# Moving two steps' shared-expert work out of the feed phase of a two-layer decoder kernel

## The chip, the cores and the metric

The kernel runs on one core of a Trainium2 chip. A core has five engines that run their own instruction streams and wait for each other on semaphores: TensorE (PE) multiplies matrices, VectorE (DVE) and ScalarE (ACT) work on tiles, GpSimd (POOL) issues indirect DMAs and does small elementwise work, and SyncE (SP) issues most of the other DMAs. PE's clock has two levels, 1.2 and 2.4 GHz; the profile shows the granted one as a share of 2.4 GHz. The metric is the device time of one launch in microseconds (us), lower is better.

## The reference, cut to what matters

The input is 4 batches of 1024 tokens with 256 features, all in fp32. Two layers run one after the other, each with a first attention, a cross attention over 77 context rows, and a mixture of experts; a layer norm follows each of the three. Only the mixture of the first layer matters here:

```
probs = softmax(x @ router_w + router_b);  tw, ti = top_k(probs, 8)      # of 64 experts
routed = sum over experts e of  cw[:, e] * (silu(x @ w1[e] + b1[e]) @ w2[e] + b2[e])
shared = sum over 2 shared experts of  silu(x @ sw1 + sb1) @ sw2 + sb2   # 256 -> 512 -> 256
x = layernorm(x + routed + shared)
```

## The kernel before, in words

The 1024 positions are cut into 8 steps of 128 positions, and a step holds those positions of all 4 batches: 512 tokens. Four phases follow each other in one instruction stream per engine.

The **first attention** (`attention_phase`, layer 0) is a software pipeline. `SEQUENCE0` lists the jobs of a round with how many rounds a step lies behind; `steady` rolls it out, so that round n works on step n for the front of the chain and on step n - 3 for its end. Rounds 8 to 10 only drain. A job has a PE part that fills a PSUM bank and an ACT or DVE part that empties it: `v`, `qk`, `kt`, `ret`, `mix`, `up` are the first attention, `wo` its output, `x1t`, `mx`, `mt`, `sc`, `pv`, `wout` the cross attention, `x2t`, `rt`, `rank` the routing, `cwt` and `b2` the experts' bias; `put` is 32 indirect DMAs on POOL that scatter a step's rows into lists by expert (L597). SP writes zeros into the lists ahead of them (L486), loads inputs, and stores each step's rows (`x2s`, L493).

The **shared experts** are cut into units. A unit is one block of 128 of the 1024 hidden features for one step: `inward` (L110, 2 matmuls of 512 columns, 4 records in the trace), a Silu on ACT (L118) and `outward` (L127, 4 matmuls of 256 columns, 8 records), which adds into PSUM over the 8 units of a step. There are 8 units in a step and 64 in all. `with_units` puts the first step's 8 units into rounds 9 and 10.

The **feed** (`feed_phase`) does the routed experts: 80 quads of 4 pages of 128 rows. A quad is a 512 KB load from the lists (L1504), 8 transposes (L1716), 16 first matmuls (L1728), 8 second matmuls (L1739), weights copied by DVE (L1633, L1638), and a 512 KB store (L1508). `feed_order` writes the order of all engines: 20 units ahead of the first quad (`FIRST_UNITS`), then one unit behind four of five quads from quad 24 on until unit 64; behind 6 of 7 quads from quad 26 on one of the 64 "sums", which add one eighth of a step's gathered results (POOL gathers L1441, DVE adds L1456). When a step's 8 units are done, DVE adds them to the step's rows (`base`, L1697), SP stores those (`send_base`, L1517) and loads the next (L1513). The first `send` also issues the load of `w2` (L1520, twice 4 MB). All of this stands in SP's order ahead of the loads of the first quad. The other weights `w1` (4 MB, L2133) are loaded at the start of the kernel.

The **second attention** (layer 1) begins when the last quad's results are stored. Its DVE and POOL streams first do 3 of the 18 sums left by the feed (`LATE`), the other 15 and the last norm are put by `with_late` behind jobs of rounds 0 to 5. The last phase, layer 1's mixture, is not touched.

Of the kernel before, what the change touches and what calls it, by code (L numbers as in the profile page):

```python
# [26 lines left out]
K0 = 8  # L27
# [5 lines left out]
TOTAL = STEPS * UNITS  # L33
# [44 lines left out]
class SharedExperts:  # L78
# [16 lines left out]
    def load_rows(self, sp, src_t, s):  # L95
        for b in range(NB):
            at = b * SEQ + s * P
            sp.dma_start(self.sx[:, s % 2, :, b * P:(b + 1) * P],
                         src_t[:, at:at + P].rearrange("(c p) n -> p c n", p=P)).then_inc(self.sx_in[s % 2], 16)

    def inward(self, nc, pe, n, sp_h):
        s, u = n // UNITS, n % UNITS
        if n == 0:
            pe.wait_ge(self.sw1_in, 16 * ES)
# [16 lines left out]
    def outward(self, nc, pe, n, sp_y):  # L121
        u = n % UNITS
        if n == 0:
            pe.wait_ge(self.sw2_in, 16)
# [40 lines left out]
def steady(sequence):  # L165

    order = []
    for n in range(STEPS + max(ahead for _, ahead, _ in sequence)):
        for stage, ahead, part in sequence:
            if 0 <= n - ahead < STEPS:  # L170
# [33 lines left out]
def bank_jobs(order):  # L204
# [5 lines left out]
    ("wout", 2, 0), ("wout", 2, 1), ("cwt", 3, 0), ("put", 3, 1), ("qk", 0, 0), ("x1t", 1, 0), ("x1t", 1, 1),  # L210
# [17 lines left out]
def attention_phase(nc, sems, shared, layer, d, src, src_t, dst, dst_t, experts, prefetch, lists, slots, weights, page_ends,  # L228
                    spare=None, route=None, block=None,
                    over=(), kept=(), late_on_pool=None, late_on_vector=None, units=None):  # L230
# [17 lines left out]
    with ExitStack() as ctx:  # L248
# [61 lines left out]
        if first:  # L310
# [25 lines left out]
            qt = x1t  # L336
        else:
            xt, qt = (units.sw2[:].rearrange("p (k c n) m -> p k c (n m)", k=2, c=KC)[:, k] for k in range(2))
# [26 lines left out]
            placed = sb("placed", [P, NB, K1, E])  # L365

# [20 lines left out]
        if first:  # L387
# [3 lines left out]
            blank = [sem(f"blank{i}") for i in range(STEPS)]  # L391
        else:
# [63 lines left out]
        def _(sp):  # L456
# [23 lines left out]
            prefetch(sp, 0)  # L480
            if first:
                sp.wait_ge(pool_ready, 3)
            out_rows = dst.rearrange("(b s) n -> s b n", b=NB)
            for n in range(STEPS + 3 if first else 0):
# [3 lines left out]
                if n == 1:  # L488
                    sp.dma_start(units.sb1[:], d["sb1"]).then_inc(units.sb1_in, 16)
                if 0 <= n - 3 < STEPS:  # L490
# [15 lines left out]
                if n + 2 < STEPS:  # L506
                    filled(sp, ("v", n, 1))
                    filled(sp, ("qk", n, 3))
                    load_t(n + 2)
                if n == STEPS - 1:  # L510
# [7 lines left out]
                    sp.wait_ge(sent_cols, 64 * 2)  # L518
                    for k in range(2):
                        units.load_rows(sp, dst_t, k)  # L520
                if 0 <= n - 2 < STEPS:
# [3 lines left out]
                    sp.dma_start(route[n - 2, 0], place[:].rearrange("p b e -> p (b e)")).then_inc(sent_place, 16)  # L525
            for n in range(0 if first else STEPS + 3):
# [88 lines left out]
        def _(act):  # L615
            def move(out, in_, job):
                empties(nc.scalar.activation(out, in_, ACT.Copy), job)

            begin_here(act)
            for dst_ap, src_ap in others:  # L620
                act.dma_start(dst_ap, src_ap).then_inc(consts, 16)
            if not first:
                act.wait_ge(consts, CONSTS)
                nc.scalar.activation(small[:, 0:1], gate[:], ACT.Exp, scale=-1.0).then_inc(gate_exp, 1)
            for job in order:
                stage, i, p = job
                pair = slice(2 * p, 2 * p + 2)
                if stage == "unit":
                    units.activate(nc, act, i, wide[:, 0])
                if stage in ("v", "kt"):  # L630
# [56 lines left out]
        def _(dve):  # L687
# [81 lines left out]
            if not first:  # L769
                lay_out()  # L770
            for job in order:
# [151 lines left out]
                if stage == "rank":  # L923
# [38 lines left out]
                    if i + 1 < STEPS:  # L962
                        dve.wait_ge(mask_done, i + 1)
                        step(nc.vector.tensor_copy(counts[:, 0], counts[:, NB]))
                if stage == "b2":
# [8 lines left out]
        def _(pe):  # L974
# [16 lines left out]

            begin_here(pe)
# [17 lines left out]
            for job in order:  # L1010
# [3 lines left out]
                if first and job == ("mx", 0, 0):  # L1014
                    pe.wait_ge(ready, READY)
                if stage == "unit":
# [213 lines left out]
                if stage == "rank":  # L1230
# [6 lines left out]
                    fills(ins, job)  # L1237
                if stage == "cwt":
# [986 lines left out]
```

## Time and profile before

| | us |
|---|---|
| timed runs | 1865.97, 1873.0, 1875.45; median 1873.0 |
| profiled execution, first to last instruction | 1981.9 |
| profiled execution's own time beside its span | the page gives none |
| PE / DVE / ACT / POOL busy in it | 1687.5 / 1165.2 / 623.2 / 892.7 |
| mean granted clock of PE | 0.922 |
| DMA traffic | 322.61 MB, mean 163 GB/s |

The page cuts the span into 40 slices of 49.5 us. The first attention takes slices 1 to 12, the feed ends near 1105 us, the second attention near 1560 us, and the last phase takes the rest. In the feed's slices PE is busy 8 to 9 tenths and the DMA engines 8 to 9 tenths as well. The chain of work that ended last is 68% PE, 10% DVE, 6% DMA and 6% issue.

### The profile page before, as it was taken

Reading aid. Unit: us, or ns where it says so; the run is one execution under the profiler, and the core shown is the slowest. Engines: PE = TensorE matmul, PEld = TensorE weight load, DVE = VectorE, ACT = ScalarE, POOL = GpSimd, SP = SyncE. Lnnn points to the kernel's source line nnn. Section 1 sums busy time; section 2 is a strip of 40 time slices with the busy share of each in tenths; the row PEclk is TensorE's granted clock in tenths of the full one; section 3 lists DMA queues with packets and bytes.
Section 4 is the critical chain, followed back from the end, with each engine's and each line's share of the span. In section 5 each row is a group of like instructions: output and inputs, shape, how many; then the busy total and the mean of one; then the engine's idle time right before and its main releaser. Section 6 shows DMA issues by size and latency. Waiting matters only on the chain.

```text
span 1981.9 us, 45543 instructions
## 1 busy us (share of the span) xinstructions
PE 1687.5 (85%) x17739; PEld 1329.8 (67%) x17739; DVE 1165.2 (59%) x3228; ACT 623.2 (31%) x957; POOL 892.7 (45%) x1000
## 2 busy tenths in 40 slices
PE   6788888887689889998998478889977599999994
PEld 4566665666566567666676355667666499999994
DVE  4576655665432177776656456788765245655564
ACT  1232322222231277454555223445432111111110
POOL 0017556655758102888888856333323102222223
PEclk9999989998689999999998779999987699999997
DMA  9416543555448899888998922113111512333332
GB/s 325 150 46 199 184 150 116 190 169 191 146 147 237 219 304 295 285 278 273 297 294 290 317 78 82 57 65 121 69 39 65 164 49 76 91 94 98 98 94 69
DMA packets 269634, 322.61 MB, mean 163 GB/s; under 512 B 25083, under 2 KB 245487, under 8 KB 268655
## 3 DMA queue, kind: packets, MB, share of 16 engines
q1 hardware_dynamic: 234559, 226.38, 36.1%
q0 software_dynamic: 33024, 92.32, 14.4%
q8 instruction: 144, 2.36, 0.5%
q10 hardware_dynamic: 1840, 1.00, 0.2%
q14 instruction: 67, 0.55, 0.1%
HBM read 157.22 MB, written 162.40 MB: 161 GB/s over the span
## 4 chain that ended last, share of the span: by engine, by line
PE 68%; DVE 10%; issue 6%; DMA 6%; ACT 4%; POOL 3%; another core or an unknown queue 2%; SPq 1%; DVEq 1%; POOLq 0%; ACTq 0%
PE wide L2067 13%; PE d_yp L2079 6%; PE wide L110 4%; PE wide L127 4%; PE wide L1199 4%; PE wide L1202 3%; PE wide L1728 3%; PE e_yp L1739 3%; PE wide L1186 3%; PE bank L1033 3%; PE bank L1212 3%; PE bank L1219 2%; PE e_xp L1716 2%; PE bank L1105 2%
## 5 line engine op out<-in xcount | busy, mean ns | idle before, releaser
L1441 POOL DMA_INDIRECT big<-results,slots x256 | 263.4, 1029 | 202.1 <-DMA results<-e_y 125.5
L2067 PE MATMUL wide<-d_xt,d_ws 128*128 128x128 f32 x2272 | 279.0, 277 | 0.6 <-issue 0.6
L2067 PEld LDWEIGHTS wide<-d_xt,d_ws 128*128 128x128 f32 x2272 | 272.7, 193 | 4.5 <-issue 1.0
L597 POOL DMA_INDIRECT lists<-big,slots x160 | 159.6, 997 | 116.7 <-DVE slots L961 70.3
L663 ACT ACTIVATE pt<-wide 77x2048 f32<-77x2048 f32 x64 | 119.8, 1871 | 196.5 <-PE wide L1202 118.7
L1936 POOL DMA_INDIRECT d_picked<-results,slots x64 | 64.0, 1001 | 182.0 <-DMA results<-d_y 168.7
L1967 ACT ACTIVATE d_gate<-wide 128x512 f32<-128x512 f32 x71 | 42.4, 597 | 323.9 <-PE wide L2067 323.9
L2079 PE MATMUL d_yp<-d_wd,d_h 128*128 x568 | 134.2, 379 | 0.0
L1456 DVE SCALAR_TENSOR_TENSOR big<-big,weights 128x256 f32<-128x256 f32 x256 | 108.9, 487 | 41.6 <-DMA big<-results,slots 28.2
L110 PE MATMUL wide<-shared_sx,shared_sw 128*128 128x512 f32 x256 | 126.3, 616 | 7.7 <-DMA shared_sx<-res_t 5.2
L127 PEld LDWEIGHTS wide<-shared_sw,shared_sh 128*128 128x128 f32 x512 | 97.3, 191 | 45.1 <-issue 29.6
L127 PE MATMUL wide<-shared_sw,shared_sh 128*128 128x256 f32 x512 | 121.4, 380 | 3.6 <-DVE big L1697 3.6
L158 POOL TENSOR_TENSOR rest_ones<-rest_ones 128x4 f32<-128x4 f32 x108 | 121.0, 1120 | 2.0
L554 POOL TENSOR_TENSOR rs<-mv,eps 128x4 f32<-128x4 f32 x32 | 6.4, 199 | 234.9 <-DVE mv L712 234.1
L1212 PE MATMUL bank<-pt,vals 77*32 77x128 f32 x2048 | 89.6, 293 | 25.3 <-issue 15.4
L2079 PEld LDWEIGHTS d_yp<-d_wd,d_h 128*128 128x128 f32 x568 | 102.6, 190 | 11.0
L1998 DVE COPY d_ws<-big 128x1024 f32 x142 | 92.3, 693 | 27.5 <-issue 26.4
L2016 DVE TENSOR_TENSOR d_h<-d_gate,wide 128x512 f32<-128x512 f32 x71 | 48.7, 686 | 97.7 <-PE wide L2067 97.7
L1587 ACT ACTIVATE e_xt<-e_xp 128x1024 f32<-128x1024 f32 x80 | 81.9, 1024 | 76.5 <-PE e_xp L1716 48.7
L1716 PE MATMUL e_xp<-e_ident,e_x 128*128 128x128 f32 x640 | 86.9, 280 | 15.8 <-DMA e_x<-lists 12.2
L1199 PE MATMUL wide<-x1t,keys 32*77 32x128 f32 x1024 | 69.7, 315 | 35.8 <-issue 13.6
L1728 PE MATMUL wide<-e_xt,e_w1s 128*64 128x128 f32 x1280 | 89.4, 283 | 12.5 <-DVE e_w1s L1633 11.0
(280 smaller groups left out, 3488.8 us busy)
## 6 DMA issues: line engine op xcount, KB each, us to landing
lists<-zero SPq DMA_DIRECT2D x20, 2048.0 KB, 14.6
e_x<-lists SPq DMA_DIRECT2D x80, 512.0 KB
results<-e_y SPq DMA_DIRECT2D x80, 512.0 KB
d_x<-lists SPq DMA_DIRECT2D x71, 128.0 KB
results<-d_y SPq DMA_DIRECT2D x71, 128.0 KB
e_w<-in_L_w SPq DMA_DIRECT2D x2, 4096.0 KB
shared_sw<-in_x_t SPq DMA_DIRECT2D x32, 128.0 KB
x<-in_x SPq DMA_DIRECT2D x8, 512.0 KB
```

Source lines behind the costliest of these rows:

```text
L110: ins = nc.tensor.matmul(sp_h, self.sw1[:, c, u * P:(u + 1) * P], self.sx[:, s % 2, c], start=c == 0, stop=c == KC - 1)
L127: ins = nc.tensor.matmul(sp_y[b // 2][:, b % 2 * DM:(b % 2 + 1) * DM], self.sh[:, n % 2, b * P:(b + 1) * P], self.sw2[:, u], start=u == 0 ...
L158: step(self.nc.gpsimd.tensor_tensor(self.ones[:, 1], self.ones[:, 0], self.ones[:, 0], ALU.pow))
L597: pool.indirect_dma_start(out=lists, out_offset=bass.IndirectOffsetOnAxis(ap=slots[:, b, i, k:k + 1], axis=0), in_=z2[i % 3][:, b, :], in_ ...
L663: empties(nc.scalar.activation(pt[0:CTX, p % 2].rearrange("k (j n) -> k j n", j=4), ps[0:CTX], ACT.Exp, scale=score_scale), job)
L1199: mm(out[0:CTX, r, n * P:(n + 1) * P], keys[quarter(r), p, c, h * CTX:(h + 1) * CTX], qt[quarter(r), c, toks(p)], start=True, stop=False, ...
L1212: ins = mm(out[quarter(r), at:at + P], vals[:, p, c * 8 + 2 * r + h], pt[0:CTX, p % 2, of:of + P], start=True, stop=True)
L1441: pool.indirect_dma_start(out=picked[:, c % NG, b, :], out_offset=None, in_=results[0:-(-PAGES_OF_STEP[s] // 4) * 4 * R0, :], in_offset=ba ...
L1716: ins = tr(xp[:, h, (a * KC + c) * P:(a * KC + c + 1) * P], x[:, j % NX, h, a, c * P:(c + 1) * P], ident[:])
L1728: ins = mm(hp[h * H0:(h + 1) * H0, a * R0:(a + 1) * R0], w1s[:, j % NW1, h, a, c], xt[:, j % 2, h, a, c], start=c == 0, stop=c == KC - 1)
L2067: ins = mm(out[T % 2][:, a * P:(a + 1) * P], ws[:, T % NW, n, c, a * P:(a + 1) * P], xt[:, T % 2, c], start=c == 0, stop=c == KC - 1)
L2079: ins = mm(yp[T % 2][:, 0:DM], h[:, T % 2, c * P:(c + 1) * P], wd_flat[:, bass.ds(e * (HC * DM) + c * DM, DM)], start=c == 0, stop=c == HC ...
```

## The change: what it does

The first step leaves the units: its 8 units become 8 jobs `win` (inward and Silu) and 4 jobs `wtwo` (outward for two batches and four units each) of the first attention, all in round 8 except two `wtwo` in round 9. They use the four narrow PSUM banks, and DVE adds their result to a copy of the step's rows (`gbase`), which SP stores. Their weights are loaded in round 1 into the memory that `w1` had; so the load of `w1` moves from the start to the end of SP's round 9, behind the last `wtwo`.

The other seven steps have 56 units. The first 8 stay in rounds 9 and 10, 13 (was 20) come ahead of the first quad, and the feed goes on to unit 48; units 49 to 55 and the last outward run on PE behind the last quad, ahead of the second attention, where DVE then adds them and SP stores them. So quads 59 to 79 have no unit, where 70 to 79 had none. The sums come behind 7 of 9 quads instead of 6 of 7, and 22 (was 18) are left to the second attention, whose `xt` and `qt` get memory of their own.

```diff
+SOON = 1
+FOUR = UNITS // 2
+GROUPS = SOON * UNITS // FOUR
+TOTAL = (STEPS - SOON) * UNITS
+IN_FEED = TOTAL - UNITS
...
-    behind = [("x0t", 0, 1), ("sig", 0, 0)]
+    behind = [("x0t", 0, 1), ("sig", 0, 0), ("num", 0, 1), ("x0t", 1, 1), ("sig", 1, 0)]
     for i in range(4):
-        behind += [("x1t", i, 1), ("q", i, 1), ("mx", i, 1), ("mx", i, 3)]
+        behind += [("num", i + 1, 1), ("x1t", i, 1), ("q", i, 1), ("mx", i, 1), ("mx", i, 3)]
...
+    ("wout", 2, 0), ("wout", 2, 1), ("wtwo", 9, 10), ("wtwo", 9, 11), ("win", 8, 0), ("cwt", 3, 0), ("put", 3, 1),
+    ("win", 8, 1), ("qk", 0, 0), ("x1t", 1, 0), ("x1t", 1, 1), ("win", 8, 2),
+    ("mx", 1, 0), ("ln2", 2, 0), ("qk", 0, 1), ("b2", 3, 0), ("b2", 3, 1), ("mx", 1, 1), ("win", 8, 3), ("res", 1, 0), ("put", 3, 2),
+    ("qk", 0, 2), ("x2t", 2, 0), ("x2t", 2, 1), ("mx", 1, 2), ("win", 8, 10), ("put", 3, 3), ("qk", 0, 3), ("mx", 1, 3),
+    ("win", 8, 11), ("put", 3, 4), ...
+    ("sc", 1, 0), ("wtwo", 8, 0), ("mix", 0, 0), ("top", 2, 0), ("ret", 0, 1), ("pv", 1, 0), ("sc", 1, 1), ("wtwo", 8, 1),
+    ("mix", 0, 1), ("up", 0, 0), ("rank", 2, 0), ("sc", 1, 2), ("pv", 1, 1), ("sc", 1, 3), ("win", 8, 12), ("pv", 1, 2),
+    ("win", 8, 13), ("pv", 1, 3),
...
-            prefetch(sp, 0)
             if first:
                 sp.wait_ge(pool_ready, 3)
+            else:
+                prefetch(sp, 0)
+                last_units.send(sp)
...
+                    sp.dma_start(gw2, d["sw2"].rearrange("e (c p) n -> p (e c) n", p=P)).then_inc(units.sw2_in, 16)
...
+                if n == 4:
+                    sp.wait_ge(sent_cols, 64)
+                    load_group(0)
+                    load_gbase(0)
...
+                if n == STEPS + 1:
+                    filled(sp, ("wtwo", GROUPS - 1, 1))
+                    prefetch(sp, 0)
+                    send_gbase(0)
...
+            if not first:
+                for n in range(IN_FEED + 1, IN_FEED + 3):
+                    units.activate(nc, act, n, wide[:, 0])
             begin_here(act)
             for dst_ap, src_ap in others:
                 act.dma_start(dst_ap, src_ap).then_inc(consts, 16)
             if not first:
+                for n in range(IN_FEED + 3, TOTAL):
+                    units.activate(nc, act, n, wide[:, 0])
...
             if not first:
+                last_units.add_base(dve)
                 lay_out()
...
+            if not first:
+                for n in range(IN_FEED + 1, TOTAL + 1):
+                    if n < TOTAL:
+                        units.inward(nc, pe, n, wide[:, 0])
+                    if n == IN_FEED + 1:
+                        last_units.begin(pe)
+                    units.outward(nc, pe, n - 1, [wide[:, 1], wide[:, 2]])
             begin_here(pe)
...
+                if stage == "win":
...
+                    for c in range(KC):
+                        ins = mm(out[:], gw1[:, c, u * P:(u + 1) * P], gx[:, c], start=c == 0, stop=c == KC - 1)
+                    fills(ins, job)
+                if stage == "wtwo":
+                    for n in range(FOUR):
+                        emptied(pe, ("win", i, n))
+                    for bb in range(2):
+                        for n in range(FOUR):
+                            u = i % 2 * FOUR + n
+                            ins = mm(out[:, bb * DM:(bb + 1) * DM], gh[:, u, toks(2 * p + bb)], gw2[:, u],
+                                     start=n == 0, stop=n == FOUR - 1)
+                    fills(ins, job)
...
-LATE = STEPS * K0 - 18
+LATE = STEPS * K0 - 22
 AHEAD = 3
-FIRST_UNITS = 20
+FIRST_UNITS = 13
...
-            if unit[0] <= TOTAL:
+            if unit[0] <= IN_FEED:
...
-        if j >= begun + 2 and (j - begun) % 7:
+        if j >= begun + 2 and (j - begun) % 9 < 7:
             sums(1)
```

## Rows read from the trace of the kernel before

**Rows 1.** Windows: length, busy PE, PEld, DVE, ACT, POOL; PE clock, DMA share, GB/s

```profile
417.80:485.00 67.20, 56.41 (x834) 42.46 (x831) 41.34 (x104) 18.66 (x25) 40.34 (x45) 0.92 0.60 192
485.00:558.40 73.40, 53.10 (x537) 39.78 (x534) 34.24 (x98) 15.40 (x19) 47.10 (x52) 0.68 0.61 202
...
685.00:767.00 82.00, 72.19 (x734) 55.27 (x736) 57.02 (x189) 59.72 (x91) 0.00 (x0) 1.00 0.91 294
...
986.00:1105.00 119.00, 106.69 (x821) 77.86 (x818) 71.62 (x262) 61.98 (x96) 98.06 (x95) 0.96 0.90 287
1105.00:1129.00 24.00, 0.03 (x1) 0.06 (x1) 7.58 (x23) 2.51 (x3) 19.43 (x21) 0.52 1.00 305
```

**Rows 2.** Groups by line of PE in round 7, 417.8 to 485

```profile
L1033 PE MATMUL bank<-shared_sw,wqk 128*128 128x512 f32 x16 | 7.8, 612 | 0.0
...
L1069 PE MATMUL bank<-shared_sw,state 128*32 128x128 f32 x64 | 5.3, 294 | 1.4 <-issue 1.3
L1074 PE MATMUL bank<-big,shared_sx 128*32 128x128 f32 x64 | 5.0, 281 | 0.7 <-issue 0.6
...
L1039 PE MATMUL bank<-wv,shared_sw 128*128 128x256 f32 x16 | 3.6, 379 | 0.0
```

**Rows 3.** Timeline of PE: last wout of the first attention, and two units ahead of quads

```profile
558.41 5.99 PE L1219 MATMUL bank<-wout,att_t 128*128 128x256 f32 x16
...
614.25 1.88 PE L110 MATMUL wide<-shared_sx,shared_sw 128*128 128x512 f32 x4
...
617.69 1.88 PE L110 MATMUL wide<-shared_sx,shared_sw 128*128 128x512 f32 x4
```

**Rows 4.** Chain of waits between the first attention and the first quad

```profile
597.41 2.95 DMA res<-x2s
...
611.07 1.30 DVE big L1697 x2
...
680.16 4.89 DMA e_x<-lists
```

**Rows 5.** Timeline of SP in the same stretch: start, time of issue

```profile
615.74 15.92 SPq L1520 DMA_DIRECT2D e_w<-in_L_w  x2
633.81 26.10 SPq L98 DMA_DIRECT2D shared_sx<-res_t  x4
659.96 2.23 SPq L1517 DMA_DIRECT2D mid<-big  x1
669.50 0.36 SPq L1513 DMA_DIRECT2D big<-res  x1
```

**Rows 6.** Timeline of POOL: the last scatter of the last step

```profile
654.00 0.96 POOL L1572 DMA_INDIRECT lists<-big,slots  x1 [0.30 <-issue]
```

**Rows 7.** Chain of waits in the feed's last third

```profile
1046.53 0.87 PE e_xp L1716 x8
1047.41 1.02 PE wide L1728 x16
...
1053.14 0.87 PE e_xp L1716 x8
...
1072.48 1.98 PE wide L1728 x16
```

**Rows 8.** Timeline of ACT, DVE and PE between the feed and the second attention

```profile
1117.58 1.28 ACT L624 ACT_TABLE_LOAD   x1 [11.52 <-issue]
...
1125.96 1.67 DVE L1456 SCALAR_TENSOR_TENSOR big<-big,weights 128x256 f32<-128x256 f32 x4 [5.36 <-DMA big<-mid]
...
1128.97 1.96 PE L1001 MATMUL bank<-pt,wk 128*128 128x77 f32 x8 [24.04 <-DMA memory<-in_L_norm]
```

**Rows 9.** Chain of waits in the second attention: its wout jobs

```profile
1279.13 1.92 PE bank L1219 x8
...
1324.72 1.92 PE bank L1219 x8
...
1365.46 1.92 PE bank L1219 x8
```

More of the change, by code:

```diff
@@ L169, in steady @@
         for stage, ahead, part in sequence:
-            if 0 <= n - ahead < STEPS:
+            if stage in ("win", "wtwo"):
+                if n == ahead:
+                    order.append((stage, part // 10, part % 10))
+            elif 0 <= n - ahead < STEPS:
                 order.append((stage, n - ahead, part))
@@ L489, in _ @@
                     sp.dma_start(units.sb1[:], d["sb1"]).then_inc(units.sb1_in, 16)
+                    sp.dma_start(gw2, d["sw2"].rearrange("e (c p) n -> p (e c) n", p=P)).then_inc(units.sw2_in, 16)
+                    for e in range(ES):
+                        sp.dma_start(gw1[:, :, e * HS:(e + 1) * HS], d["sw1"][e].rearrange("(c p) n -> p c n", p=P))\
+                            .then_inc(units.sw1_in, 16)
                 if 0 <= n - 3 < STEPS:
@@ L629, in _ @@
                     units.activate(nc, act, i, wide[:, 0])
+                if stage == "win":
+                    u, at = i % 2 * FOUR + p, i % 2 * FOUR + p
+                    if i == 0 and p == 0:
+                        act.wait_ge(units.sb1_in, 16)
+                    if i >= 2 and p == 0:
+                        filled(act, ("wtwo", i - 2, 1))
+                    ps = filled(act, job)
+                    empties(nc.scalar.activation(gh[:, at], ps[:], ACT.Silu, bias=units.sb1[:, u:u + 1]), job)
                 if stage in ("v", "kt"):
@@ L1015, in _ @@
                     pe.wait_ge(ready, READY)
+                if not first and job == ("mx", 0, 0):
+                    last_units.end(pe)
                 if stage == "unit":
@@ L1237, in _ @@
                     fills(ins, job)
+                if stage == "win":
+                    u = i % 2 * FOUR + p
+                    if i == 0 and p == 0:
+                        pe.wait_ge(units.sw1_in, 16 * ES)
+                        pe.wait_ge(units.sw2_in, 16)
+                    if i % 2 == 0 and p == 0:
+                        pe.wait_ge(gx_in, 64 * (i // 2 + 1))
+                    for c in range(KC):
+                        ins = mm(out[:], gw1[:, c, u * P:(u + 1) * P], gx[:, c], start=c == 0, stop=c == KC - 1)
+                    fills(ins, job)
+                if stage == "wtwo":
+                    for n in range(FOUR):
[6 more added lines that the diff above has]
+                    fills(ins, job)
                 if stage == "cwt":
@@ L1479, in norm, with begin, end, add_base @@
             ins.then_inc(out_done, 1)
+        class LastUnits:
+            def begin(self, pe):
+                pe.wait_ge(sy_used, STEPS - SOON - 1)
+            def end(self, pe):
+                pe.wait_ge(sy_used, STEPS - SOON)
+            def add_base(self, dve):
+                base_on_vector(dve, STEPS - SOON - 1)
+            def send(self, sp):
+                base_on_sync(sp, STEPS - SOON - 1)
+        def base_on_vector(dve, n):
+            dve.wait_ge(base_in, 16 * (n + 1))
+            dve.wait_ge(experts.out_full, n + 1)
+            for k in range(2):
+                pair = slice(2 * k, 2 * k + 2)
+                ins = nc.vector.tensor_tensor(base[:, pair], sp_y[k][:].rearrange("p (b n) -> p b n", b=2),
+                                              base[:, pair], ALU.add)
+            ins.then_inc(sy_used, 1)
+        def base_on_sync(sp, s):
+            sp.wait_ge(sy_used, s + 1)
+            sp.dma_start(out_by_step[(SOON + s) * P:(SOON + s + 1) * P], base).then_inc(base_sent, 16)
         def late_on_pool(pool, n):
```

84 lines of the change are left out of this document (54 added, 30 removed), and 5 rows, old and new, of the table SEQUENCE0.

## The prediction, written before the changed kernel ran

> **What bounds the kernel now.** I read the windows first, cut at the phases' ends, then PE's groups and timelines inside a phase, then the chain of waits and SP's timeline where PE stands still. Four stretches matter.
>
> Round 8 of the first attention is a drain: it lasts 73.4 us although PE has less to do than in round 7, which takes 67.2. PE is busy for 53.1 us of it, but at a granted clock of 0.68, against 56.4 us at 0.92 in round 7 [rows 1]. So this round is short of work, and its work runs slowly: what ends waits there is a chain through PE, ACT and DVE.
>
> Between the first attention and the first quad (the head, 596 to 685), PE does 20 units at 3.44 us each (617.69 - 614.25) [rows 3], but the first quad is not held by PE alone. SP stands in `w2`: issued at 615.74, it leaves no room in SP's queue for the next small load, whose issue takes 26.1 us, to 659.9. Only then come the store of a step's rows and its landing, at 669.5 [rows 5], another step's rows that wait for unit 24, and at 680.16 the first quad's load, 4.9 us [rows 4]. The scatters on POOL end at 655.0 [rows 6], so they are not what ends last.
>
> In the feed a quad with a unit takes 6.61 us (1053.14 - 1046.53) at the full clock [rows 7], and this is PE's own time. Quads without a unit are carried by the DMAs: the first 24 take 82.0 us at 294 GB/s and a DMA share of 0.91, with PE at 72.2 busy. The last third, 986 to 1105, moves 287 GB/s at 0.90 with PE busy for 106.7 of 119 us [rows 1]. So two limits lie close together there.
>
> From 1105 to 1129 PE does nothing [rows 1]; it waits 24.04 us for the second attention's constants [rows 8].
>
> **The change part by part.** The sum is against the profiled execution's span, 1981.9 us. The page gives no time around it, and the timed median is 1873.0, 5.5% below. Which stages the profiling stretches no view shows; I carry the difference over in microseconds.
>
> *Rounds 8 and 9.* Round 8 gets eight `win`, each the first half of a unit, 1.72 us, and two `wtwo` of 3.44: 13.8 + 6.9 = 20.7 us of PE. Round 7 has the jobs of round 8 and in their place `qk`, `v` and `mix`, which alone are 7.8 + 3.6 + 5.3 + 5.0 = 21.7 us [rows 2]. So round 8 becomes a round like 7, which is the nearest row: 67.2 + 1 for Silu's tables, about 5 us less than now. The `wout` behind it is at the low clock now, 5.99 us for 16 [rows 3], where 8 take 1.92 at the full one [rows 9]: 2 us more. Together -7. Ends: all 20.7 us on top and the clock as it is, +21; or 53.1 x 0.68 + 20.7 = 57 us and no idle, -16. Two more `wtwo` in round 9 put 6.9 us ahead of `rank`, of which I let 3 fall into waits: +4 for SP, nothing for POOL, whose scatters follow `wout`.
>
> *The early loads.* `w1` leaves the start, two smaller weights and a step's columns come. PE's work there never waits for them in the chain; I cost it at nothing, with 3 us either way if the saturated first stretch matters.
>
> *The head.* SP's `x2s` store is issued at 597.41 and lands in 2.95 [rows 4]; with -7 and +4 it is issued at 594.4. But now 4.19 MB of `w1` stand just ahead of it in SP's queue. At the 305 GB/s of a window with DMA share 1.00 [rows 1] that is 13.7 us; at the pace of `w2`, which takes 44.2 us (659.96 - 615.74) for twice as much beside the scatters [rows 5], 22. It is contiguous, so I take 14: it lands at 611.4. DVE's plan and the first base follow that store, now 12.0 us behind it (to 612.37) [rows 4], so 623.4, and `w2` 3.4 us later, 626.8. The scatters end at 648. Up to there `w2` moves 8.39 / 44.2 = 0.19 MB per us, 4.0 MB; the other 4.4 MB at 0.294 [rows 1] take 15: 663. The store of the second step's rows and its landing take 9.5 as now (669.50 - 659.96) [rows 5]: 672.5. With 13 units the third step's send is no longer ahead of the quads, so their load follows at 673 and lands at 678, against 685.05: -7 for the whole stretch up to the first quad. PE waits for the first base, then does 12 units, 41.3 us, until 665; it does not hold the quad. The seven units taken from here are 24 us of PE, but only the send counts. Ends: -18 with round 8 at its best, +14 with none of it hidden and `w1` at 22.
>
> *The feed's quads.* Quads 24 to 58 keep their pattern of units. Then 8.5 units leave the quads from 59 on: 29.2 us of PE. What is late next is the DMAs. That stretch moves 119 x 0.287 = 34.2 MB; two gathers and a step's rows in and out fewer, 2.6 MB, leave 31.6 MB, at the 294 GB/s of the unitless quads 107.5 us: -11.5. POOL, 98.1 us busy for the 18 sums there [rows 1], has 16, about 87, and is not the limit. Ends: -29 when the DMAs give way, and +13 when the clock falls (below).
>
> At this place the Trainium skill says otherwise: in DMA: Bandwidth & Descriptors, section Where 436 GB/s comes from, transfers between HBM and SBUF are held by the memory side at about 358 GB/s per core. By it the 31.6 MB would take 88 us (an estimate from that page) and the whole 29 us of PE would come out; the trace shows 294 at a share of 0.91, so I stay with that.
>
> *The change-over.* Seven inwards and eight outwards, 7.5 units or 25.8 us, go into PE's 24 us of waiting. They begin when PE ends, at 1104.9. The first three run; unit 52 needs the Silu of 51, which on ACT stands behind the wait for the last store and the issue of the constants, to 1117.6 [rows 8], so PE waits some 3 us: 1104.9 + 25.8 + 3 = 1134. The keys start there instead of 1128.97: +5. DVE's sums, up to 1127.6 [rows 8], are over by then; the last base is added at 1135, and the layout goes along with the keys. On SP the send of the last rows stands behind loads that are issued anyway. Ends: 0, if the warm clock gives the keys back, and +26, if none is hidden.
>
> *The late sums.* Two successive rounds of the second attention take 45.6 (1324.72 - 1279.13) and 40.7 us (1365.46 - 1324.72) [rows 9], the first with four more sums: 1.2 us each, so +4 for four. Each also puts a gather on POOL, but spread over five rounds. Ends +1 and +8.
>
> Sum: -7 - 11.5 + 5 + 4 = -9.5, so 1972.4 for the profiled span and **1863.5** for the median.
>
> **The rivals.**
>
> *The DMAs give way.* Without units the quads follow PE, and the feed loses all 29.2 us. For it: the last third is already at a share of 0.90 with PE nearly full, so the share is no proof of a limit. Against: the first 24 quads have no units and no gathers, and are at 294 GB/s. -7 - 29.2 + 5 + 4 = -27: 1846. The figure of the Trainium skill above would end there.
>
> *SP's queue eats the head.* `w1` moves at the pace of `w2`, 8 us more, and round 8 gains nothing, since its waits are of ACT's and DVE's making: the first quad comes 4 us later than now instead of 7 earlier. For it: 26.1 us of a small load's issue behind `w2` [rows 5]. Against: `w1` has long contiguous rows. +4 - 11.5 + 5 + 4 = +1.5: 1874.5.
>
> *The clock falls in the quads without units: slower.* PE has 3.2 us of work per quad (6.61 - 3.44) against 5.1 of the DMAs (107.5 / 21), and at 1072 to 1074 the trace has a stretch where the 16 first matmuls take 1.98 us instead of 1.02 [rows 7]. At the low clock a quad is 6.3 us of PE: 21 of them 132 us, not 107.5, and the units behind the last quad take twice 25.8. That is +50 for all of it. It decides from the point where the low level holds for a quarter of the stretch; at half, +25, the sum is +15.5: 1888.5. Against: in the first 24 quads PE is 88% busy and the clock stays at 1.00 [rows 1], so the fall feeds on waits longer than those.
>
> **How the numbers follow.** About 0.5%, 9.4 us, is what a measurement of this kernel can tell from no change. The forecast has 0.45, with an own range of 1853 to 1872 and somewhat more than half of it below 1863.6; the DMAs giving way 0.20, SP's queue 0.20, the clock 0.15. Faster by over 0.5%: 0.25 + 0.20 + 0.02 = 0.47. Within: 0.18 + 0.15 + 0.03 = 0.36. Slower: 0.02 + 0.03 + 0.12 = 0.17. The range takes in the first rival's 1846 and most of the third's way to 1888: 1845 to 1882.
>
> **What would show it.** Round 8 of the changed kernel at about 68 us with a granted clock near 0.9; `w1` issued just ahead of `x2s`, and that store landing some 14 us later behind it; the load of the first quad close behind the second base's store, some 10 us after the end of `w2` instead of 20; quads 59 to 79 at 5.1 us each with the DMA share at 0.9 or above; the keys some 29 us behind the last quad; rounds 2 to 4 of the second attention a little longer. The forecast is wrong if round 8 grows, if the quads from 59 on are below 4.5 or above 5.7 us, or if the units behind the last quad run at the low clock.

## The result, and the profile after

The changed kernel takes 1900.55 us (median of 4 runs, 1894.29 to 1903.04) against 1874.22 for the kernel before on the same chip: a ratio of 1.0149, 95% interval 1.0115 to 1.0183. It is slower by 1.5%, where 1863.5 was forecast, and outside the range that ended at 1882.

Its profiled execution has a span of 1900.4 us at 1902.2 us of device time, so 1.8 us lie around the span. That shows what was wrong with the profile of before: its span of 1981.9 lies 109 us above the timed median, because that execution was held up, by what no view shows. A second profile of the kernel before has a span of 1869.9, and it is the one to compare with. Of the 112 us between the two, 58 lie ahead of round 8 of the first attention, 24 between there and the last `x2s` store's issue, and 33 in the second attention, which the prediction read too [rows 9]. From the keys to the last phase, first in the profile that the prediction used, then in the second one (columns as in [rows 1]):

```profile
1128.97:1560.80 431.83, 344.59 (x4787) 256.20 (x4788) 295.88 (x955) 150.45 (x226) 182.18 (x219) 0.87 0.27 89
```

```profile
1049.60:1448.90 399.30, 322.42 (x4788) 246.73 (x4788) 296.52 (x959) 150.53 (x226) 183.85 (x221) 0.88 0.29 98
```

In the first attention, from 38.9 us to round 8, the waits of ACT show it, in the same order (columns: engine, tile, line, releaser: us in total, times, longest):

```profile
ACT pt L663 <- PE wide L1202: 71.9, 22, 11.0
ACT shared_sx L617 <- PE bank L1039: 54.8, 14, 8.3
ACT shared_sx L617 <- PE bank L1047: 50.9, 12, 15.6
ACT pt L663 <- remote: 49.5, 5, 11.7
```

```profile
ACT pt L663 <- PE wide L1202: 90.0, 26, 8.2
ACT shared_sx L617 <- PE bank L1039: 56.5, 14, 8.3
ACT shared_sx L617 <- PE bank L1047: 50.5, 14, 15.6
```

Five waits for something that the trace can only call "remote", 49.5 us, are gone; the waits on PE of the same tile are 18 us more. In the windows of the second profile, round 7 takes 56.2 us where [rows 1] have 67.2, and round 8 takes 46.0 where they have 73.4, at 0.89 of the clock and not 0.68. Then come the last third of the feed and the gap behind it:

```profile
371.00:427.20 56.20, 49.58 (x855) 38.99 (x846) 43.43 (x109) 18.90 (x25) 41.46 (x47) 1.00 0.73 238
427.20:473.20 46.00, 34.42 (x538) 29.00 (x535) 32.94 (x94) 15.18 (x19) 33.72 (x40) 0.89 0.61 201
...
905.50:1026.70 121.20, 106.76 (x821) 77.47 (x819) 72.59 (x264) 63.60 (x96) 99.33 (x97) 0.95 0.87 284
...
1026.70:1049.60 22.90, 0.05 (x3) 0.04 (x1) 6.36 (x20) 2.51 (x3) 18.93 (x20) 0.50 1.00 296
```

The same windows of the changed kernel, with the first 24 quads as third row:

```profile
368.00:423.10 55.10, 49.08 (x825) 38.71 (x823) 41.10 (x101) 18.89 (x25) 39.72 (x46) 0.97 0.63 207
...
423.10:477.40 54.30, 53.20 (x604) 38.41 (x598) 35.08 (x99) 24.08 (x30) 39.61 (x44) 0.97 0.65 210
...
612.10:696.20 84.10, 76.01 (x736) 58.17 (x736) 57.70 (x190) 59.77 (x91) 0.00 (x0) 0.95 0.89 286
...
909.90:1021.00 111.10, 82.49 (x718) 62.85 (x716) 68.08 (x254) 57.75 (x88) 86.21 (x84) 0.86 0.87 291
1021.00:1050.80 29.80, 27.83 (x94) 18.18 (x93) 6.95 (x15) 7.32 (x10) 24.53 (x29) 0.94 0.97 319
```

Cut at the same instructions, the two profiles differ so (us; "before" is the second profile):

| stretch | before | after | differs | forecast |
|---|---|---|---|---|
| start to round 8 | 427.2 | 423.1 | -4.1 | 0 |
| round 8 to the last `x2s` store's issue | 88.8 | 97.3 | +8.5 | -3 |
| from there to the first quad | 87.5 | 91.7 | +4.2 | -4 |
| quads 0 to 58 | 302.0 | 297.8 | -4.2 | 0 |
| quads 59 to 79 | 121.2 | 111.1 | -10.1 | -11.5 |
| last quad to the keys | 22.9 | 29.8 | +6.9 | +5 |
| keys to the last phase | 399.3 | 429.4 | +30.1 | +4 |
| last phase | 421.0 | 420.1 | -0.9 | 0 |

The first row is spread between runs: the profiles of all kernels below begin round 8 anywhere from 419 to 429, with and without the change. The 30 us in the second attention are as much as the whole loss, 30.5 us between these two profiles. Its windows, from the keys to `wout` of round 3, first before and then after:

```profile
1049.60:1256.50 206.90, 182.88 (x2542) 136.67 (x2542) 165.44 (x501) 83.42 (x130) 114.08 (x133) 0.90 0.30 97
```

```profile
1050.80:1283.90 233.10, 187.29 (x2543) 140.52 (x2542) 169.12 (x522) 83.54 (x130) 126.50 (x142) 0.86 0.27 84
```

No engine is full there: PE, the busiest, is at 88% before and at 80% after. The gathers of the four added sums are 12 us of POOL's busy time in a stretch that grew by 26. So it is not a load but an order. POOL's timeline in the changed kernel, at the first norm of the second attention and at the second:

```profile
1093.35 0.99 POOL L1545 DMA_INDIRECT big<-results,slots  x1 [0.30 <-issue]
1094.65 1.13 POOL L1545 DMA_INDIRECT big<-results,slots  x1 [0.31 <-issue]
1095.80 0.21 POOL L605 TENSOR_TENSOR rs<-mv,eps 128x4 f32<-128x4 f32 x1
...
1099.75 2.35 POOL L636 TENSOR_TENSOR x1b<-x,bout 128x1024 f32<-128x1024 f32 x1 [2.19 <-ACT x L738]
...
1133.93 0.96 POOL L1545 DMA_INDIRECT big<-results,slots  x1 [0.30 <-issue]
1134.91 0.21 POOL L605 TENSOR_TENSOR rs<-mv,eps 128x4 f32<-128x4 f32 x1
```

The norm's scale (`rs`) starts right behind a gather, with no wait in brackets: it was ready and stood in POOL's order. DVE had written its input `mv` 9.2 us sooner, by the groups of that tile (engine, operation, count: ns of one, first and last start):

```profile
L776 DVE BATCH_NORM_AGGREGATE mv<-stats x2: 148/148/148, 1084.9 to 1086.5; 128x2 f32<-128x6 f32 x2
```

POOL's timeline of the kernel before (second profile) at the same place:

```profile
1073.83 0.94 POOL L1441 DMA_INDIRECT big<-results,slots  x1 [0.30 <-issue]
1086.08 0.19 POOL L554 TENSOR_TENSOR rs<-mv,eps 128x4 f32<-128x4 f32 x1 [11.31 <-DVE mv L712]
```

There POOL had 11.31 us to spare. One late sum puts four gathers of about 0.95 us, with 0.3 between them, and a pause of 1.05 on POOL, at least 6.1 us in all (1068.68 to 1074.77 for the one whose last gather is shown here). Between the last quad and that norm the kernel before has 7 of them and the changed one 10: three more are 18 us, against 11.31 of room. In the changed kernel three norms stand behind gathers in this way, for 9, 9 and 13 us. What then waits, from the changed kernel's waits between the keys and round 3:

```profile
ACT x L738 <- POOL rs L608: 32.3, 3, 15.4
...
PE bank L1188 <- ACT x L738: 27.6, 3, 13.8
```

The first of these waits in the kernel before (second profile):

```profile
ACT x L674 <- POOL rs L557: 6.1, 2, 5.8
```

### The profile page after: what moved, and what is told of

Its sections match the earlier page's. It is cut to its first block, busy times and chain, and to the rows that moved or that the text cites. A ratio compares the mean times of both kernels' runs of the same rounds, so it can differ in the third digit from the quotient of the medians.

```text
span 1900.4 us, 45565 instructions
## 1 busy us (share of the span) xinstructions
PE 1623.9 (85%) x17739; PEld 1301.5 (68%) x17739; DVE 1165.9 (61%) x3230; ACT 628.7 (33%) x959; POOL 897.7 (47%) x1000
## 4 chain that ended last, share of the span: by engine, by line
PE 65%; DVE 9%; POOL 8%; DMA 7%; issue 5%; ACT 4%; SPq 1%; DVEq 0%; ACTq 0%; POOLq 0%
PE wide L2188 13%; PE d_yp L2200 6%; POOL big L1545 5%; PE wide L114 4%; PE wide L131 4%; PE bank L1116 3%; PE wide L1282 3%; PE bank L1302 3%; PE wide L1285 3%; PE e_yp L1860 2%; PE wide L1849 2%; PE wide L1269 2%; PE e_xp L1837 2%; ACT pt L727 2%; PE bank L1295 2%
## 5 line engine op out<-in xcount | busy, mean ns | idle before, releaser
L1560 DVE SCALAR_TENSOR_TENSOR big<-big,weights 128x256 f32<-128x256 f32 x256 | 106.9, 479 | 43.5 <-DMA big<-results,slots 32.9
L1837 PE MATMUL e_xp<-e_ident,e_x 128*128 128x128 f32 x640 | 92.7, 291 | 43.9 <-DMA e_x<-lists 42.5
L131 PEld LDWEIGHTS wide<-shared_sw,shared_sh 128*128 128x128 f32 x448 | 86.6, 194 | 55.5 <-issue 25.9
L131 PE MATMUL wide<-shared_sw,shared_sh 128*128 128x256 f32 x448 | 108.1, 385 | 18.9 <-DVE big L1604 18.9
L1837 PEld LDWEIGHTS e_xp<-e_ident,e_x 128*128 128x128 f32 x640 | 76.2, 149 | 66.4 <-DMA e_x<-lists 33.9
L114 PE MATMUL wide<-shared_sx,shared_sw 128*128 128x512 f32 x224 | 112.0, 624 | 3.2 <-ACT shared_sh L122 3.2
L1714 ACT ACTIVATE e_y<-e_yp 128x1024 f32<-128x1024 f32 x80 | 82.0, 1025 | 44.0 <-PE e_yp L1860 44.0
L659 POOL DMA_INDIRECT lists<-shared_sw,slots x64 | 62.3, 973 | 70.5 <-PE wide L1285 30.2
## 6 DMA issues: line engine op xcount, KB each, us to landing
lists<-zero SPq DMA_DIRECT2D x20, 2048.0 KB, 12.7
```

What stands on the lines that cost most here:

```text
L114: ins = nc.tensor.matmul(sp_h, self.sw1[:, c, u * P:(u + 1) * P], self.sx[:, s % 2, c], start=c == 0, stop=c == KC - 1)
L131: ins = nc.tensor.matmul(sp_y[b // 2][:, b % 2 * DM:(b % 2 + 1) * DM], self.sh[:, n % 2, b * P:(b + 1) * P], self.sw2[:, u], start=u == 0 ...
L1560: ins = nc.vector.scalar_tensor_tensor(out=acc[s % NA][:, b], in0=picked[:, n % NG, b], scalar=weights[:, b, s, k:k + 1], in1=acc[s % NA][ ...
L1714: return nc.scalar.activation(out, in_, ACT.Copy)
L1837: ins = tr(xp[:, h, (a * KC + c) * P:(a * KC + c + 1) * P], x[:, j % NX, h, a, c * P:(c + 1) * P], ident[:])
```

## The experiments

Each profile is cut as above; "second" is the stretch from the keys to the last phase, "feed" from the first quad to the end of the last. Ratios are to the kernel before on the same chip.

| label | late sums, places | units | time | ratio (95%) | feed | second |
|---|---|---|---|---|---|---|
| e0_before | 18, old | before | 1872.46 | | 423.2 | 399.3 |
| after | 22, new | changed | 1900.55 | 1.0149 (1.0115 to 1.0183) | 409.0 | 429.4 |
| e1_w1_sooner | 22, new | changed, `w1` sooner | 1881.79 | 1.0073 (1.0046 to 1.0100) | 399.8 | 425.6 |
| e2_late18 | 18, old | changed | 1892.09 | 1.0113 (1.0072 to 1.0153) | 427.1 | 399.2 |
| e3_first20 | 22, new | changed, 20 first | 1905.12 | 1.0177 (1.0136 to 1.0219) | 400.2 | 431.4 |
| e4_last_in_feed | 22, new | first step moved | 1899.73 | 1.0150 (1.0123 to 1.0177) | 410.6 | 432.4 |
| e6_late_spread | 22, old | changed | 1888.63 | 1.0109 (1.0076 to 1.0141) | 405.6 | 411.4 |
| e7_before_late22 | 22, new | before | 1885.09 | 1.0075 (1.0039 to 1.0111) | 411.2 | 433.8 |
| e8_both | 22, old | changed, `w1` sooner | 1873.78 | 1.0027 (1.0005 to 1.0050) | 401.9 | 416.3 |
| e9_first_step_only | 22, old | first step moved, `w1` sooner | 1869.80 | 0.9987 (0.9969 to 1.0005) | 409.1 | 413.3 |
| e10_before_spread22 | 22, old | before | 1870.06 | 0.9990 (0.9970 to 1.0009) | 408.8 | 415.8 |
| e11_before_spread20 | 20, old | before | 1874.01 | 0.9996 (0.9978 to 1.0014) | 419.8 | 405.3 |
| e12_before_places | 18, new | before | 1898.07 | 1.0139 (1.0115 to 1.0162) | 420.7 | 423.3 |

**e0_before**: the kernel before once more, for a profile.

> The kernel before, unchanged, for a second profile: the first one's span, 1981.9 us, lies 109 us above the timed median, and its rounds 3 to 8 of the first attention took 67 to 73 us where the changed kernel's take 54 to 58. If the first profile was of an execution that was held up for a reason outside the kernel, this one has a span near 1873 and rounds of about 55 us, round 8 among them, with no waits of ScalarE of 8 us and more in round 8; then round 8 had little to win, and the time of the change is to be read against this profile. If not, the rounds take 67 us again and the profiler stretches them.

It gave the second profile above, and with it the first of the two outcomes: rounds 3 to 7 take 54 to 58 us, round 8 takes 46.0.

**e1_w1_sooner**: `w1` behind the last `wtwo` in SP's order, ahead of the transposed columns' loads and `x2s`.

```diff
+                if n == STEPS + 1:
+                    filled(sp, ("wtwo", GROUPS - 1, 1))
+                    prefetch(sp, 0)
                 if 0 <= n - 3 < STEPS:
                     emptied(sp, ("b2", n - 3, 0))
...
                 if n == STEPS + 1:
-                    filled(sp, ("wtwo", GROUPS - 1, 1))
-                    prefetch(sp, 0)
                     send_gbase(0)
```

> The changed kernel with the load of w1 some 17 us sooner in SyncE's order: right behind the last wtwo, ahead of the round's stores, instead of behind the last route store. Theory 1 (w1 stands ahead of x2s in SyncE's queue, whose landing went from 2.95 to 18.15 us, and holds the whole head): x2s lands in about 4 us, the first quad comes 12 to 15 us sooner, and the time falls by 10 to 15 us, to about 1888. Theory 2 (the loss is at the change-over to the second attention, where POOL's gathers stand ahead of the first norm): the head shortens, but the time by less than 5 us.

Theory 1: by the ratios 14 us come back. SP's timeline of the changed kernel, then of this one:

```profile
519.31 0.43 SPq L2254 DMA_DIRECT2D big<-in_L_w  x1
519.85 0.44 SPq L519 DMA_DIRECT2D mid<-big  x1
520.41 0.43 SPq L535 DMA_DIRECT2D res<-x2s  x1
539.20 0.35 SPq L1652 DMA_DIRECT2D e_ident<-in_ident  x1
```

```profile
497.01 0.39 SPq L2255 DMA_DIRECT2D big<-in_L_w  x1
...
522.46 0.37 SPq L538 DMA_DIRECT2D res<-x2s  x1
527.25 0.34 SPq L1653 DMA_DIRECT2D e_ident<-in_ident  x1
```

From the issue of `x2s` to the next load on SP it is 18.8 us in the one and 4.8 in the other. The first quad comes 91.7 us behind that issue in the changed kernel and 79.4 here, 8.1 less than before. The feed is 9 us shorter too (mostly quads 24 to 58); with the late sums spread out, the same edit gave 4 (e6, e8). Why, I did not settle.

**e2_late18**: the late sums of before (18, old places, 6 of 7 quads) in the changed kernel.

```diff
-LATE = STEPS * K0 - 22
+LATE = STEPS * K0 - 18
...
-    behind = [("x0t", 0, 1), ("sig", 0, 0), ("num", 0, 1), ("x0t", 1, 1), ("sig", 1, 0)]
+    behind = [("x0t", 0, 1), ("sig", 0, 0)]
     for i in range(4):
-        behind += [("num", i + 1, 1), ("x1t", i, 1), ("q", i, 1), ("mx", i, 1), ("mx", i, 3)]
+        behind += [("x1t", i, 1), ("q", i, 1), ("mx", i, 1), ("mx", i, 3)]
...
-        if j >= begun + 2 and (j - begun) % 9 < 7:
+        if j >= begun + 2 and (j - begun) % 7:
             sums(1)
```

> The changed kernel with 18 late sums and the spread of the sums as before (behind 6 of 7 quads, and the second attention's late jobs at their old places). Theory 2 (POOL's gathers are back to back from quad 62 on, and with 22 late sums they stand ahead of the second attention's first norm): the first norm of the second attention comes about 9 us sooner behind the keys, its rounds with late sums are shorter, but the last 21 quads have 18 sums and take 6 to 10 us longer: same time within 5 us, or faster by up to 5. Theory 1 (the head's queue): no change but for what four sums cost, within 4 us either way.

The second attention is back at 399.2, as before to a tenth; with the moved units still ahead of it. But the feed grows by 18 us, to more than before, although it has nine units less than before (27 instead of 36 behind the quads); its last third takes 121.2 us, as before and 10 more than in the changed kernel. With 18 sums, the units taken out gain nothing there. The time is 0.4% less than the changed kernel's, within the intervals.

**e3_first20**: 20 units ahead of the first quad.

```diff
-FIRST_UNITS = 13
+FIRST_UNITS = 20
```

> The changed kernel with 20 units ahead of the first quad again instead of 13; so seven units fewer stand behind quads, and the units end at quad 50. Theory 1 (SyncE's queue sets the first quad, TensorE waits in the head): the third step's send comes back ahead of the first quad's load, so the first quad is 8 to 14 us later, and the quads without units, 29 instead of 21, win little as POOL's gathers hold them: slower by 5 to 12 us. Rival (the head has room, and TensorE bounds the quads): first quad no later, quads 24 us shorter: faster by 10 to 20 us.

Seven units more, 24 us of PE at 3.44 each, put the first quad 11.4 us later behind `x2s` (103.1 against 91.7) and take 8.8 out of the feed. In its chain the last unit on PE ends at 626.5, where the quad's transposes begin. So PE's units do hold the first quad. The time is the changed kernel's within the intervals.

**e4_last_in_feed**: the last step's units back in the feed, ahead of the last quads.

```diff
-IN_FEED = TOTAL - UNITS
+IN_FEED = TOTAL
```

(with the parts of `last_units` left out)

> The changed kernel with the last step's units put back into the feed (ahead of its last quads), all else as changed. Theory 1 (the 30 us lost in the second attention come from the four further late sums on POOL): the stretch from the keys to the gated experts stays at about 429 us; the feed's last part gets back some 10 us (111 to about 121), the change-over gives back 7 (30 to 23): about 1904 us, ratio to the kernel before about 1.016. Theory 2 (the units behind the last quad are what hold up the second attention: their activations and base additions stand ahead of its first work): that stretch falls to about 400 us, and the time to about 1875, ratio about 1.00.

Theory 1 as to the second attention (432.4). The change-over gives back 10 (19.4 against 29.8), and the feed is at 410.6 against 409.0, where 10 more had been expected. So taking these 8 units out of the feed bought 2 us there and cost 10 behind it; the time is the same within the intervals. (e8 and e9 below differ by the same edit: 7 and 10.)

**e6_late_spread**: 22 late sums, four to a round as before, into a fifth round.

```diff
-    behind = [("x0t", 0, 1), ("sig", 0, 0), ("num", 0, 1), ("x0t", 1, 1), ("sig", 1, 0)]
-    for i in range(4):
-        behind += [("num", i + 1, 1), ("x1t", i, 1), ("q", i, 1), ("mx", i, 1), ("mx", i, 3)]
+    behind = [("x0t", 0, 1), ("sig", 0, 0)]
+    for i in range(5):
+        behind += [("x1t", i, 1), ("q", i, 1), ("mx", i, 1), ("mx", i, 3)]
```

> The changed kernel with its 22 late sums behind the places of the kernel before (four in a round), carried on into a fifth round, instead of behind five places in a round and behind num and the first x1t. Theory 1a (it is the place: four more gathers of 6.4 us stand in POOL's order ahead of the first norm, whose idle time before was only 11 us): the stretch from the keys to the gated experts falls from 429 to 400 to 405 us, the time to about 1873 to 1878, ratio 0.999 to 1.004. Theory 1b (it is the number: a gather more costs its POOL time wherever it stands in the second attention): the stretch stays near 425 to 430 us, the time at about 1896 to 1900, ratio about 1.014.

Between the two: the second attention falls by 18 of the 30 us. On POOL the first norm no longer stands behind gathers:

```profile
1064.40 0.95 POOL L1545 DMA_INDIRECT big<-results,slots  x1 [0.30 <-issue]
1081.29 0.19 POOL L605 TENSOR_TENSOR rs<-mv,eps 128x4 f32<-128x4 f32 x1 [15.94 <-DVE mv L776]
```

The 12 that stay are the number: e2, the changed kernel with 18 sums on the old places, is at 399.2.

**e7_before_late22** and **e12_before_places**: the kernel before, with the late sums of the change alone; the second with their new places, but still 18 of them.

```diff
-LATE = STEPS * K0 - 18
+LATE = STEPS * K0 - 22
...
-    behind = [("x0t", 0, 1), ("sig", 0, 0)]
+    behind = [("x0t", 0, 1), ("sig", 0, 0), ("num", 0, 1), ("x0t", 1, 1), ("sig", 1, 0)]
     for i in range(4):
-        behind += [("x1t", i, 1), ("q", i, 1), ("mx", i, 1), ("mx", i, 3)]
+        behind += [("num", i + 1, 1), ("x1t", i, 1), ("q", i, 1), ("mx", i, 1), ("mx", i, 3)]
...
-        if j >= begun + 2 and (j - begun) % 7:
+        if j >= begun + 2 and (j - begun) % 9 < 7:
```

> The kernel before with the 22 late sums in the new places alone; units and their loads as before. Theory 1: the second attention from the keys to the gated experts rises from 399 to about 428 us, and the feed with four gathers fewer falls by at most 15 us (the difference in the feed between the changed kernel with 18 and with 22 late sums): about 1874 + 29 - 15 = 1888 us, ratio 1.005 to 1.012. Theory 2 (units behind the last quad): the second attention stays at about 399 us, the feed loses up to 15 us: about 1860 us, ratio about 0.992.

> The kernel before with its 18 late sums in the new places (five in a round, from num on); number, units and loads as before. Theory 1a (place): four of the gathers more stand ahead of the first norm of the second attention on POOL, 25.6 us against 11.3 us of idle time there: the second attention rises from 399 to 413 to 425 us, the time by 14 to 25: 1885 to 1896 us, ratio 1.007 to 1.013. Theory 1b (number): second attention at 399 to 403 us, time as before, ratio 0.998 to 1.002.

Theory 1 and 1a. No unit is moved, and the second attention takes 433.8 and 423.3 us. In e12 neither the number nor the feed changes (420.7 against 423.2), and the places alone cost 24 us of the profile and 1.4% of the time:

```profile
1100.05 0.95 POOL L1441 DMA_INDIRECT big<-results,slots  x1 [0.30 <-issue]
1101.02 0.21 POOL L554 TENSOR_TENSOR rs<-mv,eps 128x4 f32<-128x4 f32 x1
```

Its `mv` was written at 1086.1: 14.8 us in POOL's order. ACT waits 32.3 us for three such norms, as in the changed kernel:

```profile
ACT x L674 <- POOL rs L557: 32.3, 3, 21.2
```

**e8_both**, **e9_first_step_only**: e6 with e1's edit; and e4 with both.

> The changed kernel with the late sums on the old places carried into a fifth round, and the load of the first feed weights issued directly behind the first step's units in SP's order instead of behind the sorted columns' loads. Theory 1a: both gains add, 1900 - 26 - 19 = about 1855 us, ratio 0.988 to 0.994. Theory 1b: only the earlier load counts, about 1881 us, ratio about 1.006.

> The changed kernel with the last step's units back in the feed, the late sums on the old places carried into a fifth round, and the first weights' load directly behind the first step's units: of the moved units only the first step's move is left. From the runs so far (first units and head 175 us with the sooner load against 176 to 179 before; change-over 19 to 20; feed behind quad 24 about 317 to 320; second attention 411 to 416): 1868 us, ratio 0.996 to 1.000. If moving the first step's units shortens the feed (theory: the feed is held by its units), the feed is at least 8 us shorter than in the run of the kernel before with 22 spread late sums; if the feed is held by POOL's gathers, both feeds agree within 5 us.

e8 ends 15 us below e6, as e1 by the ratios ends 14 below the changed kernel, but 19 above what I expected: 13 of it by the number of late sums (416.3, where I took 403), and 5 because the 19 that I took for `w1` was the difference of two times from two chips. e9 is as fast as before (interval 0.9969 to 1.0005). Its feed and e10's agree (409.1 and 408.8), but that does not decide between the two theories: the trace has 35 units in e9's feed and 36 in e10's, since the seven units taken from the head came into it. What the first step's move gains lies in the head (78.8 us behind `x2s`, against 88.5 in e10), and 6.9 of these 9.7 us go into the stretch ahead of it (97.3 against 90.4).

**e10_before_spread22**, **e11_before_spread20**: the kernel before with 22 or 20 late sums on the old places carried into a fifth round (e6's edit, `LATE` and the pattern behind the quads).

> The kernel before with 22 late sums on the old places carried into a fifth round; no unit is moved. Theory (POOL's gathers hold the feed's tail, and the places hold the second attention): the feed stays 12 us shorter, as with 22 late sums in the new places, and the second attention falls from 434 to about 411 us: 1885 - 22 = about 1863 us, ratio 0.993 to 0.998. Rival (the feed's 12 us came from the chip's spread between runs): feed as before, second attention 12 us longer, about 1883 us, ratio 1.006.

> As the run before it in this list, with 20 late sums instead of 22. If each late sum takes its gather of 6.4 us out of the feed's tail and costs less than that in the second attention, the time lies between the kernel before and the one with 22: about 1866 us, ratio 0.995 to 0.999. If the second attention has free room for two more gathers and none for four, it stays at 399 to 403 us, the feed loses 6: about 1864 us, as fast as with 22 or faster.

Four sums taken from the feed shorten it by 14.4 us and lengthen the second attention by 16.5; two, by 3.4 and 6. A late sum costs about what it saves: 0.993 to 0.998 was expected for e10 and 0.995 to 0.999 for e11, and both ratios came out above that. No version is faster than the kernel before by more than its interval.

The last third of e10's feed has the units of the kernel before in it, PE at 104 of 113 us, and is within 2 us of that of the changed kernel, where PE has 82:

```profile
901.70:1014.50 112.80, 103.78 (x821) 75.88 (x819) 68.38 (x252) 63.62 (x96) 84.91 (x84) 0.98 0.90 292
```

**The loss as a sum of parts**, by timed ratios: four more late sums on the old places -0.1% (e10); their new places +0.85 (e7 less e10; with 18 sums +1.4, e12, so the parts depend on each other); the first step's units in rounds 8 and 9, with `w1` ahead of `x2s` and 13 units first, +0.75 (e4 less e7); the last step's units behind the last quad 0.0 (the changed kernel less e4; +0.4 with the other parts mended, e8 less e9). The third part is `w1`'s place: with `w1` sooner and the sums spread it is 0.0 (e9 less e10), and that place alone gives back 0.76 (the changed kernel less e1).

## Why the prediction was wrong

**The step that failed is the late sums.** The prediction priced four sums at 1.2 us each from two rounds of one chain [rows 9] and set POOL aside: "Each also puts a gather on POOL, but spread over five rounds. Ends +1 and +8." The runs show +30. By time the new places are about half of the loss; the other half is a second step, `w1`'s load (the head, below). The term took the sums as work to be divided over rounds; what counts is which of POOL's instructions stand behind them. Three of the new places, behind `num`, `x0t` and `sig`, lie ahead of the first norm, where ACT waits for the norm and PE for ACT (32.3 and 27.6 us above). Places alone cost 24 us (e12). And even on good places a late sum costs 3 to 4 us (e10, e11), three times the 1.2; and [rows 9] lie in the second attention of the profile that was held up by 33 us there. Neither the range nor a rival had this: all three rivals lie ahead of the keys.

**Rounds 8 and 9** (-7, and +4 for SP's side): +8.5 up to `x2s`. Five profiles without the first step's units have 88.8 to 92.5 us there, eight with them 95.6 to 97.7, so +6.4 on average. The -7 came from [rows 1]: round 8 was read as stalled, 73.4 us at 0.68. In an undisturbed execution it is 46 to 53 us in five profiles without those units and 53 to 55 with them. The prediction saw that the span lay 5.5% off the median and carried the difference over as a constant; much of it lay in the very rows from which terms were read.

**The head.** `w1` ahead of `x2s` in SP's queue did as forecast: the store landed in 18.15 us instead of 2.95 [rows 4] (14 more were expected), and the 12 units behind the first base took 41.3 (550.74 to 592.06). What failed is "it does not hold the quad". In the chain of waits of the changed kernel, PE's last unit there ends at 592.06, and SP's loads of the next rows, the send and the quad's load follow it one by one:

```profile
590.33 1.73 PE wide L114 x4
592.06 1.53 SPq L102
...
597.84 8.80 DMA mid<-big
...
607.13 4.80 DMA e_x<-lists
```

The forecast had taken the 26.1 us of the small load in [rows 5] for want of room in SP's queue behind `w2`. In the same profile's chain it is a wait for a unit on PE, which has to be done with the rows before SP may load the next ones:

```profile
652.73 1.73 PE wide L110 x4
654.46 2.08 SPq L98
```

So the units held the quad before the change too, and `w1`'s delay, which keeps them waiting for the first base, went through: e1 lets the store land 14.0 us sooner, and the first quad comes 12.3 sooner behind its issue. The second rival (SP's queue eats the head) had the direction: the first quad 4 us later, where the profiles have it 12.7 later from the start of round 8 on (8.5 and 4.2). Without that delay the head is 8 to 10 us shorter than before (e1 against the second profile, e9 against e10).

**The quads from 59 on**: -11.5 forecast, -10.1 measured, so the number came out well, in part by luck. The forecast let the units' time on PE give way until the DMAs were the limit, and set POOL aside: "has 16, about 87, and is not the limit". POOL is indeed not full there (86 of 111 us), but PE comes to wait for its gathers all the same: DVE waits for them before it can add a sum, and copies the quads' weights behind that. POOL's gathers are 45% of the chain that ends last there in e2 and 33% in the changed kernel. From e2's waits in its last third:

```profile
DVE big L1560 <- DMA big<-results,slots: 33.5, 11, 6.5
...
PE wide L1849 <- DVE e_w1s L1760: 23.2, 8, 8.1
```

The traces can be sorted by the gathers that fall into these 21 quads. With 66 to 71, they take 119 to 121 us with the units in place (e0, e11, e12) and 117 and 121 without (e3, e2); e3 leaves 22 sums, but its sums came late and 68 gathers fall here. With 60 to 64, they take 112.8 to 116.3 with the units in place (e4, e7, e9, e10; mean 114.5) and 107.1 to 111.1 without (after, e1, e6, e8; mean 109.2). So the sums give some 6 us and the units 5 more, and those only behind the sums. And over the whole feed the sums alone give as much as the whole change (408.8 in e10, 409.0 in the changed kernel). Whether a gather costs by POOL's order or by its bytes is not separated: length times rate in the rows above is 34.4 MB before, 32.9 in e10 and 32.3 in the changed kernel. PE's waits there in the changed kernel say that the quads' loads are what units had covered:

```profile
PE e_xp L1837 <- DMA e_x<-lists: 17.0, 7, 6.7
```

The DMA part of the forecast had 31.6 MB at 294 GB/s, and 32.3 at 291 were moved. The Trainium skill gives about 358 GB/s per core (DMA: Bandwidth & Descriptors, section Where 436 GB/s comes from). No run reached that in this stretch: they moved 277 to 302 GB/s, the changed kernel 291 with PE at 82 of 111 us, so the traces do not bear out the rival that rested on transfers giving way. The third rival's mechanism did occur in small: the clock there is 0.86 against 0.95. In the first 24 quads, too, it is 0.95 in the changed kernel, where the forecast had 1.00.

**The change-over**: right. +6.9 for +5; the keys come 29.8 us behind the last quad, 29 were forecast. But e4 shows that it cost 10 us for 2 in the feed.

## What to carry to other kernels

Work that is put off onto an engine's in-order stream is priced by what stands behind it there and how long that has been ready, not by its own duration: look up the idle time ahead of the first urgent instruction, and count what you put in front of it. Before rows are read from a profile, compare its span with the timed median, and if they differ, find the stretch that holds the difference first. A gain seen in a stretch belongs to an edit only when that edit alone gives it: here the sums alone shorten the feed as much as the whole change, and they were the condition of what the units gave in its last third.

## What the runs showed of the hardware

A 4.19 MB load issued 1.1 us ahead of a small store in the same queue kept that store from landing for 18.15 us; issued 25.5 us ahead of it, 4.15. One execution of a program on one core was 109 us longer than the timed median, 82 of it in the first attention, with 49.5 us of ACT's waits there that its own engines don't explain, and 33 in the second. An indirect gather of 128 rows kept POOL busy for about 0.95 us with 0.3 between two, so that four with their pause took 6.1 us (second profile), and a norm that stood behind gathers in POOL's order started up to 14.8 us after its input was ready (e12). In the feed's last third, PE's busy time fell by a fifth (103.8 us in e10, 82.5 in the changed kernel) and the time by 1.5% (112.8 and 111.1).
